# VectorE's order in an edge step of a graph kernel: one-hots dealt into short runs, the low one-hots halved and made a step ahead

## The reference

```python
e = edge_feats @ W_e + b_e
m = jax.nn.relu(e + node_feats[src])
agg = jax.ops.segment_sum(m, dst, num_segments=n)
h = agg + (1.0 + eps) * node_feats        # then W1, batch norm, relu, W2
...
msg = hw[src] * norm[:, None]             # three times, hw = h @ W
agg = jax.ops.segment_sum(msg, dst, num_segments=n)
h = jax.nn.relu(agg + b)
```

## Time and profile before

| | us |
|---|---|
| median of 3 timed runs | 3148.88 (3140.8 to 3151.97) |
| the profiled execution | 3141.62 |
| its span, first to last instruction | 3139.8 |
| POOL busy, of which the gathers (L662) | 1605.2, 1598.0 |
| PE busy | 2557.4 |
| DVE busy | 2149.1 |
| ACT busy | 968.6 |

### The profile page before, as it was taken

How to read it: one execution, slowest core, us unless ns; L and a number is a source line. 1 busy time by engine, 2 the same in 40 slices (tenths; PEclk the granted TensorE clock), 3 DMA queues, 4 the chain that set the end, 5 groups by cost and what they waited for, 6 DMA issues and landing times.

```text
span 3139.8 us, 48219 instructions
## 1 busy us (share of the span) xinstructions
PE 2557.4 (81%) x16328; PEld 2238.1 (71%) x16328; DVE 2149.1 (68%) x4255; ACT 968.6 (31%) x1165; POOL 1605.2 (51%) x1582
## 2 busy tenths in 40 slices
PE   4767878777778777777778787787899999999995
PEld 4667767677667766767677776666788888888884
DVE  8767677776767676767676777765798854454446
ACT  1112222222222222222222222226555554455441
POOL 7777777777777777777777777740000000000000
PEclk9687777877777777777776777778999999999997
DMA  6444444444444444444444444432334323323332
GB/s 218 113 120 122 125 124 126 119 125 123 124 124 123 126 123 126 123 125 123 125 124 123 123 124 122 126 98 78 124 121 161 141 107 135 157 105 140 141 141 83
DMA packets 145379, 394.65 MB, mean 126 GB/s; under 512 B 36821, under 2 KB 100096, under 8 KB 139760
## 3 DMA queue, kind: packets, MB, share of 16 engines
q1 hardware_dynamic: 93298, 278.01, 24.6%
q0 software_dynamic: 50176, 102.50, 15.3%
q10 hardware_dynamic: 1662, 10.97, 0.9%
HBM read 286.56 MB, written 104.77 MB: 125 GB/s over the span
## 4 chain that ended last, share of the span: by engine, by line
POOL 48%; PE 30%; issue 15%; DVE 3%; ACT 2%; DMA 1%; DVEq 0%; SPq 0%; ACTq 0%
POOL work L662 48%; PE psE L958 13%; PE psA L958 13%; PE psA L929 1%; PE psA L901 1%; PE psS L890 1%; PE psE L823 1%; ACT wide L767 0%; PE psA L851 0%; PE psS L837 0%; DVE z L1200 0%; PE psE L885 0%; DMA work<-in_x_flat,idx 0%; ACT xn L740 0%; PE psA L885 0%
## 5 line engine op out<-in xcount | busy, mean ns | idle before, releaser
L662 POOL DMA_INDIRECT work<-in_x_flat,idx x1568 | 1598.0, 1019 | 485.7 <-issue 476.5
L823 PE MATMUL psE<-we,work 65*128 65x128 f32 x3136 | 594.4, 367 | 471.1 <-DVE work L1086 426.6
L823 PEld LDWEIGHTS psE<-we,work 65*128 65x128 f32 x3136 | 548.2, 271 | 491.0 <-DMA work<-in_edge_cols 377.6
L1086 DVE TENSOR_TENSOR work<-psE,work 128x1024 f32<-128x1024 f32 x196 | 239.9, 1224 | 557.4 <-DMA work<-in_x_flat,idx 556.7
L851 PE MATMUL psA<-z 128*128 128x245 bf16 x3136 | 582.7, 354 | 0.0
L1106 DVE TENSOR_SCALAR z<-iota_c,key,scale 128x490 bf16<-128x490 f16 x1568 | 555.1, 415 | 21.6 <-DVE z L1098 0.9
L700 ACT ACTIVATE work<-psA 128x490 int32 x392 | 227.3, 580 | 903.9 <-PE psA L851 887.6
L958 PE MATMUL psE<-wide,halves 128*128 128x500 f32 (+1 forms) x2058 | 447.9, 375 | 5.7 <-ACT halves L776 5.3
L837 PEld LDWEIGHTS psS<-onehot,work 128*128 128x128 f32 x3136 | 417.1, 214 | 38.5 <-issue 32.8
L837 PE MATMUL psS<-onehot,work 128*128 128x72 f32 x3136 | 419.6, 292 | 21.2 <-DVE acc L1118 21.2
L687 ACT ACTIVATE work<-work 128x1024 f32<-128x1024 f32 x196 | 207.2, 1057 | 733.7 <-DVE work L1086 733.6
(11 more groups left out here) (160 smaller groups left out, 1330.1 us busy)
## 6 DMA issues: line engine op xcount, KB each, us to landing
counts<-adjacency SPq DMA_DIRECT2D x36, 3062.5 KB, 9.9
adjacency<-work SPq DMA_DIRECT2D x392, 245.0 KB
work<-in_edge_cols SPq DMA_DIRECT2D x196, 256.0 KB
work<-in_x_flat,idx POOLq DMA_INDIRECT x1568
counts<-adjacency SPq DMA_DIRECT2D x3, 1592.5 KB, 6.2
acc<-in_x_cols ACTq DMA_DIRECT2D x1, 3136.0 KB, 23.2
xn<-in_x_rows ACTq DMA_DIRECT2D x1, 3136.0 KB, 32.0
x_spill<-xn SPq DMA_DIRECT2D x12, 256.0 KB, 2.3
```

What stands on the lines that cost most here:

```text
L662: gp.indirect_dma_start(gath[0:size(g), g % R, j, :], None, x_flat[:, :], bass.IndirectOffsetOnAxis(ap=idx[0:size(g), g, j:j + 1], axis=0) ...
L823: mm = pe.matmul(psE0[0:n, j, :], eaT[0:FE + 1, g % RE, j, 0:n], we[:, :], start=True, stop=True)
L1086: ve.tensor_tensor(gath[0:n, g % R, :, :], psE0[0:n, :, :], gath[0:n, g % R, :, :], ALU.add).then_inc(sum_ok, 1)
```

## The change

In the DVE order of an edge step the low one-hots are made in two halves (512 elements per partition each, one instruction of 1024 before), for step s+2 instead of s+1; the eight chunk one-hots are made in runs of 3, 2, 2 and 1 (before: 4 and 4), with a half of the low one-hots between the runs; and both banks of the step before last are taken apart after `add_window`, where before the first stood ahead of the low one-hots. In front of the loop the low one-hots of steps 0 and 1 are made.

```diff
-            def low_hots(s):
-                if s >= LB:
+            def low_hots(s, q):
+                if s >= LB and q == 0:
                     ve.wait_ge(chunk_mm, HQ * (s - LB + 1))
-                ve.tensor_tensor(lows[:, s % LB, :, :], low2[:, J * s:J * s + J].unsqueeze(2).to_broadcast([P, J, P]),
-                                 iota_c[:, 0:P].unsqueeze(1).to_broadcast([P, J, P]), ALU.is_equal).then_inc(low_ok, 1)
+                ve.tensor_tensor(lows[:, s % LB, q:q + J // 2, :], low2[:, J * s + q:J * s + q + J // 2].unsqueeze(2).to_broadcast([P, J // 2, P]),
+                                 iota_c[:, 0:P].unsqueeze(1).to_broadcast([P, J // 2, P]), ALU.is_equal).then_inc(low_ok, 1)
...
                 if k % J == 0:
-                    ve.wait_ge(low_ok, k // J + 1)
+                    ve.wait_ge(low_ok, 2 * (k // J) + 2)
...
-            low_hots(0)
+            for q in (0, J // 2):
+                low_hots(0, q)
             for i in range(J):
                 chunk_hot(i)
+            for q in (0, J // 2):
+                low_hots(1, q)
...
                     add_rows(s + 1)
                     window_hot(s + 1)
-                    if s >= 1:
-                        take_apart(2 * (s - 1))
-                    low_hots(s + 1)
-                    for i in range(4):
+                    for i in range(0, 3):
+                        chunk_hot(J * (s + 1) + i)
+                    if s + 2 < G:
+                        low_hots(s + 2, 0)
+                    for i in range(3, 5):
+                        chunk_hot(J * (s + 1) + i)
+                    if s + 2 < G:
+                        low_hots(s + 2, J // 2)
+                    for i in range(5, 7):
                         chunk_hot(J * (s + 1) + i)
...
                 add_window(s, at)
                 if s >= 1:
-                    if s + 1 == G:
-                        take_apart(2 * (s - 1))
+                    take_apart(2 * (s - 1))
+                if s + 1 < G:
+                    chunk_hot(J * (s + 1) + 7)
+                if s >= 1:
                     take_apart(2 * (s - 1) + 1)
...
-                if s + 1 < G:
-                    for i in range(4, J):
-                        chunk_hot(J * (s + 1) + i)
```

## The result

The changed kernel takes 3210.43 us (median of 5 runs, 3204.29 to 3214.93) against 3148.88: ratio 1.0205, 95% interval 1.019 to 1.022. It is slower by 62 us; 3128 was forecast, with a range up to 3205. The profiled execution took 3204.29, span 3202.5.

What follows compares the result with a forecast made beforehand. POOL's queue of 1568 gathers was taken as the bound. Loss per step falling from 0.51 to 0.39-0.40 us gave 190 x 0.11 = 21 us less: 3120.6 against the profiled 3141.6, 3128 in median terms; range 3090 to 3205.

Steps and rivals of the forecast that it cites:

- the phase: Edge step: start of L1086 after the start of the gather under way; said to decide the holds, usually 0.45 us.
- part 2: DVE's new order laid against the gathers: at phase 0.45, loss 0.39 before, 0.27 after; 0.12 us per step, 23 us.
- rival A: L1086 against the gathers: the edge goes the wrong way, slower from x = 0.33 on; 3178 to 3248; chance 0.35.
- x: Share of edge steps whose L1086 starts short of the edge, taken as 0.2; a step loses 0.21 + 0.91x us.
- Part 4: Stores and attributes go out later, load_ea at 9.6 to 10.7 us; last gather lands in 1.6 to 1.8, not 3.3.
- Part 5: Cost of L1086's new phase, 0.03 to 0.2: loss 0.39 to 0.40 us per step against 0.51, 21 us less.
- the edge: L1086 starting just after a gather: about 1.12 us lost per step short of it, 0.12 to 0.24 beyond.
- the 0.21 of part 5: Gather loss per edge step beyond the edge in the new order: 0.21 us taken from 0.12 to 0.24.
- The rule weighed: SBUF port: VectorE's fast tensor_scalar locks GpSimd out until it ends; a tensor_tensor is inferred not to stall descriptor generation.
- rival C: SBUF port: only tensor_scalars hold gathers, 0.17 before and 0.27 after at phase 0.45; +19 us, 3168; chance 0.05.
- B: Rival: the phase stays, as the last gather's landing remains 3.3 us; -23 us, 3126; chance 0.13.
- D: Rival: nothing measurable, x about a third or port holds given back as longer issue; 3149; chance 0.17.

Runs made afterwards that it cites:

- x_after: The changed kernel run again with no edit, in a group where the kernel before took 3147 us: 3214.77 us, ratio 1.0211.
- z_delay: The changed kernel with a useless copy from PSUM into a dead tile put ahead of each L1086: 3140.02 us, ratio 0.9975 to the kernel before.
- y_halves_alone: The kernel before with only the low one-hots made as two adjacent halves, same step and place: 3519.64 us, ratio 0.9952, at the 3530 level.

## Why the prediction was wrong

The bound and the gathers' queue were right, and so was the phase as something that decides; part 2's layout of VectorE's new order was met within 0.03 us in the step above (its last instruction ends 7.15 after L1086 starts, 7.16 forecast). The sign was rival A's, but not by its mechanism: at the measured x its formula gives 0.21 + 0.91 x 0.31 = 0.49 us per step, no change at all. A term was mis-sized.

- **Part 4 was right on the order of events and half right on the landing.** The load goes out 8.98 us after L1086 (median; 6.84 before; the forecast 9.6 to 10.7 was too late), PE waits for it and POOL doesn't, and where it goes out after the last gather's end that gather lands in 1.6 or 1.9. But I took one new landing, 1.6 to 1.8. There are three (1.6, 1.9, 3.4), because the load keeps its distance to L1086 while the last gather ends 7.3, 8.5 or 9.8 after it, as the phase has it: 69, 53 and 44 steps.
- **Part 5, the edge:** x was 0.2 and came out as 58 of 189, 0.31 (x_after 0.36). The price short of it was 1.12 and is 1.35.
- **The step that failed is the 0.21 of part 5, the loss beyond the edge**, and behind it part 2. Steps beyond the edge lose three times that: (189 x 0.902 - 58 x 1.40) / 131 = 0.68, with 0.902 the mean of all steps and 1.40 that of the 58. Part 2 had the order 0.12 us cheaper at equal phase; the table has it dearer by 0.07 to 0.28 at all phases beyond 0.3, and by 0.66 at 0.1 to 0.2. For the new order at phases of 0.1 to 0.3 part 2 had 0.12 to 0.32; that is met only from 0.26 to 0.30, and up to 0.25 the loss is 0.91 or more, as both take_aparts hold a gather. At 0.45 its working gave 0.39 for before, measured 0.39, and 0.27 for after, measured 0.50. I had counted a gather's first ask alone and let it wait for the instruction under way. The holds of after show two: one held at the first ends 0.82 after what held it (L1092, 704.47 to 705.22, gather to 706.03), one held at the second ends 0.12 after the end of a take_apart's second half (L1114), having waited through both halves. So a take_apart that is met this way costs 0.39 to 0.52, not 0.25, and the changed kernel has 176 such gathers in its 196 steps: most of the 0.68.
- **Shares.** With the medians of the table, the kernel before loses 0.52 at its own phases; its phases with the order of after (0.38 taken for the mixed row) give 0.68; after at its own gives 0.87. By this route the order costs 0.16 us per step and the phase 0.19, 31 and 35 us over 189 steps. The split isn't unique. By the other route, after's phases with the order of before, the table gives 0.81: 0.29 for the phase (55 us) and 0.06 for the order (11 us), because short of the edge the old order is the dearer one, 1.87 against 1.35 (from 8 steps). Both add up to 66; the means, 0.62 before and 0.90 after, are 53 apart, as the rare gathers of 2.3 to 3.3 us of before are gone, and the gathers' busy time is 62 apart. The phase share rests on z_delay, which moved the phase alone; the order share on reading two orders at equal phase, not on a run that changed the order alone at this level, and its size stays open. In z_delay, at the favourable phases, the new order isn't slower than the kernel before at all.
- **The rule weighed** (the Trainium skill, SBUF — State Buffer, "Who interferes with whom"): its half on tensor_scalars holds for the take_aparts, which I undercounted, and not for the chunk one-hots, which are tensor_scalars too and hold a gather by 0.12 at most. Its inference that a tensor_tensor doesn't stall descriptor generation is again against the rows: L1092 costs 0.54 and L1098 0.31 above. I had weighed only that part: the same section also says that a VectorE instruction with two SBUF inputs contends with a GpSimd instruction that reads SBUF. The gathers read their indices (`idx`) from there, so the rows agree with that sentence, and rival C was not what the section as a whole gives. Rival C's 3168 is out, though its sign was right.
- **B and D** are out: the phase moved, and the loss is over six times 0.3%.

## What to carry to other kernels

Where two engines meet at a shared resource in a loop, the cost of an order depends on the phase between them: tabulate loss against phase from the trace before moving anything, and ask which event sets the phase. A delay of 0.34 us on an engine with slack was worth 75 us here, more than any reordering tried at that level. Breaking up a long hold is worth nothing if the last hold of the step stays where it is.

## What I had not expected of the hardware

- The same kernel before takes 3147 or 3530 us from one group of runs to another, 12% apart, each steady within 1.5% in its group. The change is 2.1% slower at the one level and 3.3% faster at the other. At 3530 POOL and L1118 wait for signals in nearly every step of the changed order (y_halves_alone: 45 and 53 of about 120) and the granted clock from 300 to 1900 us is 0.59 to 0.71, where at 3147 it is 0.73 to 0.75. What switches between the two wasn't found.
- With the load of the attributes issued at different places beside a gather, its landing comes between 1.6 and 3.4 us after its end, and not in order of distance: 2.4 us ahead gives 2.06, 1.8 ahead 2.83, 0.3 ahead 3.30, 0.45 behind 1.6. The stores move between these kernels too, and the two weren't told apart.
- Which side gets the port at the boundary of two VectorE instructions varies. In the kernel before, L1092 starts 0.08 ahead of a gather in the earlier trace rows, a take_apart follows, and it costs 0.54; in three other steps it starts 0.07 ahead, the same instructions follow, and it costs 2.33.
- Adds with one operand in PSUM (L1086, L1118) never hold a gather: the 182 gathers of the changed kernel that meet nothing else take 0.956 us at most.
